# A graph stage written out step by step, with three groups of each strip kept in SBUF

## The reference

```python
N, C = 8192, 128
h = layernorm(x)                                   # x: (N, C)
A = adj + eye(N)                                   # adj: (N, N) float32
d = sum(A, axis=1) ** -0.5
g = relu((d[:, None] * A * d[None, :]) @ (h @ W.T))
x = x + g
z = layernorm(x)
x = x + transformer_block(z)   # rmsnorm, q/k/v with rotary tables, causal attention, top-2 of 8 experts
```

## Time and profile before

| what | value |
|---|---|
| median of 3 runs | 4111.01 us (4106.96 to 4114.44) |
| the profiled execution | 4112.9 us |
| its span, first to last instruction | 4111.2 us |
| PE busy in the span | 3444.4 us (84%) |
| DVE busy in the span | 2755.8 us (67%) |
| granted clock of PE, mean | 0.916 |
| ring loads (1 MB each) | 392 |
| bytes read from HBM | 478.22 MB |

### The profile page before, as it was taken

How to read it: one execution, slowest core, us unless ns; L and a number is a source line. 1 busy time by engine, 2 the same in 40 slices (tenths; PEclk the granted TensorE clock), 3 DMA queues, 4 the chain that set the end, 5 groups by cost and what they waited for, 6 DMA issues and landing times. The chain is left out here.

```text
span 4111.2 us, 48117 instructions
## 1 busy us (share of the span) xinstructions
PE 3444.4 (84%) x16381; PEld 1321.4 (32%) x16381; DVE 2755.8 (67%) x3882; ACT 1306.3 (32%) x1635; POOL 1641.3 (40%) x1016
## 2 busy tenths in 40 slices
PE   1456899999999959988899899999889999965990
PEld 1233444444444422222222222222222222213650
DVE  7877887704444447777878877777777776515773
ACT  0000000000000013443454355454445455634660
POOL 1000000000000014544675496565558566873564
PEclk8567889999999969999999999999899999987995
DMA  9888998788887526500000000000000000002226
GB/s 377 345 344 345 348 336 328 290 300 303 285 298 282 206 101 243 209 10 4 26 19 6 5 24 13 10 1 10 1 17 15 6 1 6 6 16 85 72 69 210
DMA packets 165282, 572.71 MB, mean 139 GB/s; under 512 B 20193, under 2 KB 55786, under 8 KB 114550
## 3 DMA queue, kind: packets, MB, share of 16 engines
q1 hardware_dynamic: 91304, 457.35, 29.8%
q10 hardware_dynamic: 60432, 88.88, 6.1%
q0 software_dynamic: 13360, 24.03, 1.8%
HBM read 478.22 MB, written 90.57 MB: 138 GB/s over the span
## 5 line engine op out<-in xcount | busy, mean ns | idle before, releaser
L958 DVE TENSOR_REDUCE unit_max<-ps_max 128x1 f32<-128x512 f32 (+3 forms) x2176 | 1356.3, 662 | 422.8 <-PE ps_max L1215 306.7
L786 POOL TENSOR_TENSOR chunk_sum<-chunk_sum,probs 128x1024 f32<-128x1024 f32 (+1 forms) x528 | 1194.8, 2263 | 570.2 <-ACT probs L918 556.1
L918 ACT ACTIVATE probs<-ps_scores 128x1024 f32<-128x1024 f32 (+1 forms) x1088 | 1021.1, 984 | 1048.3 <-PE ps_scores L1234 858.8
L1215 PE MATMUL ps_max<-keep_k_stack,q_stack 96*128 96x512 f16 (+3 forms) x2176 | 762.7, 383 | 154.0 <-DVE unit_max L958 113.9
L1234 PE MATMUL ps_scores<-q_stack,keep_k_stack 97*128 97x512 f16 (+3 forms) x2176 | 617.3, 379 | 38.6 <-ACT probs L918 34.7
L1245 PE MATMUL ps_out<-probs,keep_v 128*32 128x512 f32 (+3 forms) x4352 | 567.1, 593 | 0.6 <-ACT probs L918 0.6
L314 DVE TENSOR_TENSOR partial_degree<-partial_degree,ring 128x2048 f32<-128x2048 f32 x240 | 550.0, 2292 | 7.1
L1215 PEld LDWEIGHTS ps_max<-keep_k_stack,q_stack 96*128 96x128 f16 x2176 | 182.1, 97 | 972.3 <-DVE unit_max L958 822.1
L497 PE MATMUL ps_gather<-ring,keep_attended 128*128 128x512 f32 x960 | 448.2, 629 | 22.1 <-DVE keep_attended L338 22.1
L512 PE MATMUL ps_gather_low<-ring,keep_attended 128*128 128x512 f32 x800 | 360.6, 607 | 1.4 <-DVE keep_attended L338 1.4
L277 POOL DMA_DIRECT2D scratch_lower<-lower x15 | 9.3, 618 | 815.3 <-ACT lower L416 815.3
(11 more groups left out here) (232 smaller groups left out, 2712.2 us busy)
## 6 DMA issues: line engine op xcount, KB each, us to landing
ring<-in_adj SPq DMA_DIRECT2D x392, 1024.0 KB, 7.0
scratch_slots<-empty_rows ACTq DMA_DIRECT2D x16, 2080.0 KB, 7.4
scratch_parts<-empty_part ACTq DMA_DIRECT2D x8, 2048.0 KB, 7.7
moe_parts<-scratch_parts SPq DMA_DIRECT2D x64, 256.0 KB, 4.8
moe_x_rows<-scratch_slots SPq DMA_DIRECT2D x39, 260.0 KB
x_in<-in_x SPq DMA_DIRECT2D x16, 256.0 KB, 7.0
x_in<-in_x ACTq DMA_DIRECT2D x16, 256.0 KB, 9.8
cos<-in_cos ACTq DMA_DIRECT2D x16, 256.0 KB, 7.2
```

Of the source, the lines that this page charges most:

```text
L786: nc.gpsimd.tensor_tensor(chunk_sum[:, :, lo:], chunk_sum[:, :, lo:], weights, ALU.add).then_inc(chunk_added, 1)
L918: nc.scalar.activation(probs[:, j, kv, :, lo:], ps_scores[kv][:, :, lo:], ACT.Exp, scale=SCALE).then_inc(exp_done, 1)
L958: nc.vector.tensor_reduce(unit_max[:, i, at:at + 1], bank[:, 0:width], AX_X, ALU.max).then_inc(bank_free, 1)
L1215: last = nc.tensor.matmul(out[:, 0:width], q_stack[0:SHIFT_ROW, T % QBUF, h, s * P:(s + 1) * P], k_stack[0:SHIFT_ROW, h // NREP, G * BT:G ...
```

## The change

The hardware loops are gone: the stage's steps are lists made when the program is built, and each engine's code walks through them. Four things differ in what is done.

1. *Kept groups.* Groups (t, t), (t, t+1) and (t, t+2) are loaded into six tiles of their own, in the memory that k_stack and v use later (`shared`, `keep_shared` in the order of instructions). They stay there until support of their source strip exists and are then multiplied in the first pass. The three products that read support of strip t, (t-2, t), (t-1, t) and (t, t), are called `closing(t)`; four PSUM banks hold the open sums. 347 groups are loaded in all: 256 in the first pass, and 91 again in the second.
2. *Order of loads.* A strip's groups come as: the first three below the diagonal, the far ones above it, the near ones (t, t+1) and (t, t+2), the other ones below, and the diagonal last.
3. *Degrees later.* DVE adds in two totals in turn. It scales support of strip t-1 after its third add of strip t. PE's degree sum of strip t-1 stands behind its first product of strip t. From strip 8 on, DVE first reduces the total from 2048 to 512 columns, and PE needs 4 matmuls instead of 16.
4. *Second pass.* Strips 13, 14 and 15 are complete at its start. The others are taken up in the order 0, 12, 1, 11, 2, 10, 3, 9, 4, 8, 5, 7, 6. Counted in second-pass products, strips begin to be finished at 4, 9, 14, 19, 24, 29, 34, 40, 45, 53, 58, 66, 71, 79, 85 and 92, with the turn of h four products later and the projection five. DVE adds the lower sum. x, cos and sin of strip n+1 are loaded when strip n has been rotated, since they share one buffer; x1 waits for all three. The low halves of q and k are subtracted on POOL. SP loads the lower sum of the n-th strip only after the gather of the strip two before it, in the same queue as the groups.

The core of the diff:

```diff
-    R = min(8, NB)
...
+    R = 8
+    KEPT_SPAN = 2
+    NORM_AT, SCALE_AT = 4, 2
+    LATE = NB // 2
+    stays = lambda t, s: t <= s <= t + KEPT_SPAN
+    for t in range(NB):
+        below = list(range(t))
+        order.append(below[:3] + [s for s in range(t + 1, NB) if not stays(t, s)]
+                     + [s for s in range(t + 1, NB) if stays(t, s)] + below[3:] + [t])
...
+    closing = lambda t: [(u, t) for u in range(max(t - KEPT_SPAN, 0), t + 1)]
+        if t:
+            steps_one += early[:1] + [("degrees", t - 1)] + early[1:] + closing(t - 1)
+        steps_one += later[:2] + [("turn", t)] + later[2:3] + [("support", t)] + later[3:]
+    steps_two = second_reads[:1] + [("degrees", LAST)] + second_reads[1:3] + closing(LAST) + second_reads[3:]
...
+                if earlier is not None:
+                    before, was_again = earlier
+                    if not was_again:
+                        sp.wait_ge(group_summed, summed[before])
+                    if was_again or before[1] not in again[before[0]]:
+                        sp.wait_ge(group_multiplied, produced[before])
+                sp.dma_start(tile_of[g, is_again], adj[g[0], g[1]]).then_inc(loaded_by[g, is_again][0], 16)
...
+            for n, t in enumerate(resumed):
+                if n >= 2:
+                    sp.wait_ge(strip_gathered, n - 1)
+                sp.dma_start(lower[n % 2][:], dram["lower"][t]).then_inc(lower_loaded[n % 2], 16)
...
+                    if t and n == SCALE_AT:
+                        scale_support(t - 1)
...
+                    if n == NORM_AT + 1:
+                        dve.wait_ge(std_ready, t + 1)
...
+                if t >= LATE:
+                    nc.vector.tensor_reduce(reduced[t % 2][:], partial_degree[t % 2].rearrange("p (c t) -> p t c", c=SUB),
...
-                dve.wait_ge(degree_root, strip + 1)
...
+            for t in range(NB):
+                if t:
+                    root_degrees(t - 1)
+                if t > KEPT_SPAN:
+                    spill(t - 1 - KEPT_SPAN)
+                act.wait_ge(var_ready, t + 1)
...
+                act.wait_ge(high_ready, n + 1)
+                if n + 1 < NB:
+                    load_strip(n + 1)
```

More of the change, by code:

```diff
@@ new lines, in graph_stage @@
+    is_group = lambda step: not isinstance(step[0], str)
+    ended = {t: len(second_reads) - 1 - [g[0] for g in reversed(second_reads)].index(t) + 1 for t in resumed}
+    whole = [t for t in range(NB) if not again[t]]
+    ended |= {t: 3 for t in whole}
+    finished = sorted(range(NB), key=lambda t: (ended[t], t))
+    begins = []
+    for t in finished:
+        begins.append(max(ended[t] + 1, begins[-1] + 5 if begins else 0))
+    products = [g for g in steps_one + steps_two if is_group(g)]
@@ L246, in _ @@
[L246 to L250 removed]
+            load_x(0)
+            for t in range(NB):
+                for n, s in enumerate(order[t]):
+                    load_group((t, s), False)
+                    if n == NB - 4 and t < LAST:
+                        load_x(t + 1)
@@ L563, in _ @@
[L563 to L572 removed]
+            pieces = {"degrees": sum_degrees, "turn": turn_norm, "support": find_support}
```

531 lines of the change are left out of this document (274 added, 257 removed).

## The result

The changed kernel takes **4074.3 us** (median of 5 runs, 4066.2 to 4085.3) against 4108.5 us for the kernel before on the same chip (4106.1 to 4114.4): a ratio of 0.991, 95% interval 0.990 to 0.993, so 0.9% faster. The forecast was 4063 us. On a second chip it was 4075.0 us, ratio 0.989 (0.987 to 0.992). The profiled run is the slowest of the five, 4085.3 us with a span of 4083.5.

A forecast was written before the change was run, and what follows sets the result against it. Bound: VectorE's serial work plus the degree chain in early strips, PE in late strips and the second pass. Second pass starts at 849 us and takes 579; stage ends at 1428 against 1476.5, giving 4063 us (range 3985 to 4130).

The forecast's parts named there:

- Early strips: First pass, strips 1 to 7: mean 43.9 us a strip (bounds 41.4 and 49.4) instead of 49.4.
- The waits of VectorE: First pass, early strips: new waits of VectorE, behind ACT's queue and PE's degrees, of 0 to 3.5 us a strip.
- the wait for the degree root is gone: Sign in the early strips: VectorE's idle piece of 7.46 us a strip, waiting for the root of the degrees, disappears.
- The DMA share of 1.0: Sign in the first pass: DMA share near 1.0 (at 420 GB/s) from 100 to 350 us.
- Late strips: First pass, strips 8 to 15: PE needs 3.43(t+3) + 2.7 us for strip t, plus stalls; second pass starts at 849.
- A stall: SP stops at near loads until kept slots are read: PE loses 9.1 us in each of strips 8 to 13, 5.3 in 14.
- no stall: Rival: SP's lead covers the kept slots in the late strips, 60 us go, 4003 us; chance 0.11.
- Second pass: From 849 to the stage's end at 1428: 579 us against 636 before, as 43 + 480 + 15 + 41.
- The formula 21.2 + L: Second pass: chain per strip from first rotation to projections, 21.2 us plus load time L, taken as 10 us.
- long loads: Rival in the second pass: x, cos and sin take 17.4 us to land, total 4168 us; chance 0.17.
- The clock: PE at half clock behind idle time: 2.5 us lost per late-strip stall, 3 us per chain wait in the second pass.
- The rival estimate of 4089 us: Early strips limited by HBM at about 358 GB/s: 47.6 us a strip; a small part of a rival's 0.11.

The follow-up runs named there:

- Experiment 4: Changed kernel, but group (t, t-1) is never among a strip's first three loads; in strips 1 to 3 it moves behind the near ones: 4065.0 us, ratio 0.986.
- experiment 1: Changed kernel, but SP loads a strip's two near groups behind its other groups below the diagonal, just ahead of the diagonal: 4008.3 us, ratio 0.973.
- experiment 8: Changed kernel with near loads later, (t, t-1) never among first three, lower sums loaded behind groups, x loaded earlier on its own semaphore: 3869.7 and 3867.4 us.
- experiment 7: Changed kernel with near loads behind a strip's other groups, and one near group kept instead of two (361 loads): 3988.2 us, ratio 0.968.
- experiment 3: Changed kernel, but x has its own semaphore and is loaded once z of the strip before is there: 3985.0 us, ratio 0.967.

## Why the prediction came out as it did

Direction, size and most of the steps held; 4063 was 11 us under the median, and 20 under the profiled run (4085.3 against 4065). Of these 20, 15.7 are in the early strips and 5 behind the stage, where nothing was changed and where runs differ by more than that.

- *Early strips: the term that was mis-sized.* I took 43.9 us as the mean of strips 1 to 7, between 41.4 and 49.4; they took 46.9, and strip 0 took 42.4. The waits of VectorE are what I had too small: 0 to 3.5 us a strip, 2.5 in the sum, and they are 5.9. Without them 41.0 are left, where I had 41.4. The two roots take 3.4 us of the 5.9, which is inside the forecast, so my sign that the wait for the degree root is gone was wrong: it fell to 2.2 us a strip. Loads take the other 2.5, and the forecast had nothing for them. The DMA share of 1.0 that I expected from 100 to 350 us came only at 200 (0.97); before that the queue stands for the slot of (t,t-1). I had gone through the kept slots' release for the late strips, and not through the ring's for the early ones: a group's slot comes free by PE's order, and its place in the queue is SP's order, and the two disagree about (t,t-1). Experiment 4 moves it, and strips 1 to 4 come to 42.8 on average. In strips 5 to 7 it is the near loads, whose stall I had from strip 8 on only; experiment 1 brings these strips from 44.1, 45.4 and 48.7 us to 41.2, 43.9 and 44.1. With both moved (experiment 8) strips 1 to 7 take 42.5 on average.
- *Late strips: right.* From strip 8's start to the second pass I had 484 us, measured 484.1. closing(7) ends 29.2 us into strip 8 (26 forecast), the way to the end of closing(14) takes 412.6 (415), and the rest 42.3 (42.7). A stall costs 6.6 us of idle time and 2.3 by the clock on average, 8.9 for 9.1, and the reduction takes 3.69 us, which is inside the 2.7 to 5.4 given and hidden. Experiment 1 shows the stall as cause: without it the same way is 59.0 us shorter, where the rival "no stall" had 60. It gains 15 us more ahead of closing(7), which that rival did not have.
- *Second pass: 579 forecast, 579.1 measured.* Up to the first projection it is 46.0 us for 43, the 14 intervals 477.5 for 480, the rest 55.6 for 56. The formula 21.2 + L, with the clock's cost as measured strip by strip, gives each of the eleven intervals that the chain bounds within 0.3 us (one of them with the 5.3 us of the starved group). But the agreement of the sum owes something to luck: I took one L = 10 from a trace in which loads took 4 to 18 us, and the strips took either 5 to 7 or 15 to 23. In those eleven L averages 11.0 and the clock costs 2.0, where I had 10 and 3. Since intervals are linear in L where the chain bounds, only its mean enters; had the long ones fallen on the strips of spacing 8, where PE's own 32.6 us cover up to L = 10, less would have been seen. That bursts set L was not in the forecast. Its argument against long loads, that the ring asks for only five groups in 34 us, is true on average and false in the 20 us that count.
- *The clock.* Each stall's price was put together from an idle time and a loss behind it. The loss was 2.3 us for 2.5 in the late strips and 2.2 for 3 behind the ten longer waits of the second pass. Its size is the least certain part of a single stall: it ran from 1.5 to 3.0 behind idle times that were all 6.5 to 6.8 us long.
- *Bandwidth.* The rival estimate of 4089 us rested on about 358 GB/s, from the Trainium skill, "DMA: Bandwidth & Descriptors", Specifications. That row divides a stack's 716 GB/s by two cores, and this kernel runs on one. The trace does not agree with it as a limit here: 390 GB/s over 100 us in the changed kernel, 370 over the 768 us of the first pass of experiment 7.

What stays open: why the part behind the stage takes between 2612 and 2651 us in kernels that do not differ there, and why the clock's loss differs behind stalls of one length. Neither carries a verdict.

## What to carry to other kernels

Where one queue issues loads in order, each load's place has to follow the order in which its *slot comes free*, not the order in which its data is wanted; the loads whose slots come late go last. When work is moved from one pass to another, its price is set by whether the engine has idle time there: the same 14 products cost 23 us in one pass and 4.5 in the other, and 41 once the second pass had been repaired. Where one wait takes in several loads, split it by who wants them first: x asked for earlier and on its own was worth 100 us here (both together).

## What the runs showed of the hardware

- How long a small load takes depended on the large loads still under way. In the changed kernel's second pass x (256 KB, issued by ACT) landed 2.6 to 3.0 us after its issue in the eight strips where none of SP's 1 MB loads was under way, 5.2 to 6.0 us in the five with one to three, and 13.6 to 16.3 us in the three with four or five. The count is not the whole of it: with all four edits two were under way in fifteen strips, and x took 6.0 to 17.2 us.
- A reduction over 2048 columns whose reads step 2 KB takes 3.69 us, against 0.69 for 512 columns: 1.3 times as much a column. The Trainium skill, "SBUF — State Buffer", Specifications (TRN2), names 16-byte cachelines with a penalty for each crossing; the row agrees in direction, and no run here separates it from other reasons.
- A VectorE operation with two inputs in SBUF (x1) took 0.69 us alone and 1.53 beside POOL's subtractions.
- Behind idle times of 6.5 to 6.8 us (strips 6 to 13) PE's next two products took 8.6 to 10.1 us instead of 7.03. In the second pass the turn of h and one product took 1.6 to 2.9 us longer behind idle times of 3.0 to 20.9 us, and 1.6 of these behind the longest, so the loss did not grow with the idle time. Behind idle times of 1.0 us (experiment 3) nothing was lost. 16 matmuls with one column, with no idle time at all, cost 1.4 to 1.7 us behind them as well.
